# A gated cross attention block on one Trainium2 core: the feed forward of the first three batches is worked into the last two attention units

## The reference

```python
def attention(query, kv):                       # per batch
    q = (query @ Wq + bq).reshape(B, L, 8, 4, 128)
    k, v = jnp.split(kv @ Wkv + bkv, 2, axis=-1)    # 8 heads of 128 each
    scores = jnp.einsum('blkgd,bmkd->bkglm', q, k) * scale
    attn = jax.nn.softmax(scores, axis=-1)
    return jnp.einsum('bkglm,bmkd->blkgd', attn, v).reshape(B, L, 4096) @ Wo + bo

def feed_forward(x):
    base = jnp.einsum('bsd,od->bso', x, base_W)
    probs = softmax(jnp.einsum('bsd,ed->bse', x, router_W))
    top_vals, top_idx = jax.lax.top_k(probs, 2)
    rw = top_vals / sum(top_vals)               # spread to w_dense over the 8 experts
    mid = jnp.einsum('bsd,edr->bser', x, lora_A) * w_dense[..., None]
    return base + 2 * jnp.einsum('bser,erd->bsd', mid, lora_B)

x = x + tanh(g_xattn) * attention(layernorm(x), ctx)
x = x + tanh(g_ffn) * feed_forward(layernorm(x))
```

## Time and profile before

| | us |
|---|---|
| median of 3 runs (lowest to highest) | 2341.92 (2341.48 to 2342.7) |
| the profiled execution | 2345.07 |
| its span in the profile | 2342.9 |
| PE busy | 2292.4 (98%) |
| DVE, ACT, POOL busy | 1827.5, 1686.1, 1622.5 |

### The profile page before, as it was taken

How to read it: one execution, slowest core, us unless ns; L and a number is a source line. 1 busy time by engine, 2 the same in 40 slices (tenths; PEclk the granted TensorE clock), 3 DMA queues, 4 the chain that set the end, 5 groups by cost and what they waited for, 6 DMA issues and landing times.

```text
span 2342.9 us, 37753 instructions
## 1 busy us (share of the span) xinstructions
PE 2292.4 (98%) x12568; PEld 1960.6 (84%) x12568; DVE 1827.5 (78%) x3167; ACT 1686.1 (72%) x3208; POOL 1622.5 (69%) x1367
## 2 busy tenths in 40 slices
PE   7999999999999999999999999999999999999988
PEld 6888888888888888888888888888888888888864
DVE  5887888879778787877778778787878778778775
ACT  4776777767777776777767777776777777777663
POOL 5897887967657786866757777774865667675651
PEclk9999999999999999999999999999999999999999
DMA  7444334454133233335123243323423222122211
GB/s 255 138 145 149 114 126 146 139 194 149 59 124 113 93 122 99 99 107 185 66 97 109 73 133 114 104 89 132 142 65 109 73 72 91 51 85 73 82 37 54
DMA packets 122591, 258.11 MB, mean 110 GB/s; under 512 B 13344, under 2 KB 46624, under 8 KB 122144
## 3 DMA queue, kind: packets, MB, share of 16 engines
q1 hardware_dynamic: 122400, 255.71, 32.3%
HBM read 188.81 MB, written 66.86 MB: 109 GB/s over the span
## 4 chain that ended last, share of the span: by engine, by line
PE 87%; DVE 5%; POOL 4%; ACT 2%; issue 2%; DMA 0%; ACTq 0%; SPq 0%; POOLq 0%; DVEq 0%
PE psW L362 13%; PE psW L363 12%; PE psW L364 12%; PE psW L544 7%; PE psS L364 7%; PE psS L362 7%; PE psS L363 7%; PE psW L546 7%; PE psW L545 7%; PE psW L417 2%; PE psW L425 2%; POOL xs L731 2%; POOL pl L735 1%; PE psW L462 1%; DVE mrun L1132 1%
## 5 line engine op out<-in xcount | busy, mean ns | idle before, releaser
L731 POOL TENSOR_TENSOR xs<-xs,mb 128x512 f32<-128x512 f32 (+1 forms) x832 | 1066.2, 1311 | 535.2 <-ACT mb L795 535.2
L1132 DVE TENSOR_TENSOR mrun<-psS,mrun 128x512 f32<-128x512 f32 (+1 forms) x704 | 483.4, 687 | 379.2 <-ACT xs L795 376.3
L795 ACT ACTIVATE xs<-psS 128x512 f32<-128x512 f32 (+1 forms) x832 | 497.5, 598 | 213.9 <-PE psS L364 204.1
L887 ACT ACTIVATE ph<-xs 128x512 fp32r<-128x512 f32 (+1 forms) x832 | 520.5, 626 | 0.0
L947 DVE TENSOR_TENSOR pl<-psP,ph 128x512 fp32r<-128x512 f32 (+1 forms) x674 | 460.0, 682 | 56.3 <-ACT ph L887 50.5
L1156 DVE TENSOR_TENSOR psum_<-psP,psum_ 128x512 f32<-128x512 f32 (+1 forms) x674 | 457.5, 679 | 0.0
L884 ACT ACTIVATE psP<-xs 128x512 f32<-128x512 f32 (+1 forms) x674 | 403.5, 599 | 3.2 <-DVE psum_ L1156 1.7
L362 PE MATMUL psS<-ql,kh 128*128 128x512 f32 (+1 forms) x832 | 344.7, 414 | 4.2 <-DVE mrun L1132 3.2
L544 PE MATMUL psW<-ph,vh 128*128 128x512 f32 (+1 forms) x832 | 336.1, 404 | 4.5 <-POOL pl L735 3.1
L363 PE MATMUL psS<-qh,kh 128*128 128x512 f32 (+1 forms) x832 | 328.1, 394 | 0.0
L545 PE MATMUL psW<-pl,vh 128*128 128x512 f32 (+1 forms) x832 | 328.1, 394 | 0.0
(11 more groups left out here) (155 smaller groups left out, 4564.0 us busy)
## 6 DMA issues: line engine op xcount, KB each, us to landing
wqh<-scr_wq SPq DMA_DIRECT2D x96, 256.0 KB, 2.6
wql<-scr_wq SPq DMA_DIRECT2D x96, 256.0 KB, 3.0
woh<-scr_wo SPq DMA_DIRECT2D x48, 512.0 KB, 3.2
wol<-scr_wo SPq DMA_DIRECT2D x48, 512.0 KB, 4.3
scr_wq<-wqh SPq DMA_DIRECT2D x32, 256.0 KB, 2.0
scr_wq<-wql SPq DMA_DIRECT2D x32, 256.0 KB, 2.5
scr_wo<-woh SPq DMA_DIRECT2D x16, 512.0 KB, 2.6
scr_wo<-wol SPq DMA_DIRECT2D x16, 512.0 KB, 4.0
```

Source lines behind the costliest of these rows:

```text
L731: eng.tensor_tensor(tile, tile, mb[0:rows_of(t), U % 2, :], ALU.subtract).then_inc(s_sub)
L795: return eng.activation(hi, src, ACT.Copy)
L887: eng.activation(ph[0:rows, T % RP, :], xs[0:rows, T % RX, :], ACT.Exp).then_inc(s_h)
L1132: eng.tensor_tensor(run, psS[0:rows, s % 2, :], a, ALU.max).then_inc(s_m)
```

## The change

- Unit 63 gives its first three tiles to GpSimd, as the units before it do. Their pair lies in the staging tensor `stg`. GpSimd merges unit 62's pair after the subtraction S7 of unit 63, no longer after S1, and DVE adds unit 63's own pair after its last tile.
- Tiles 0 to 5 of the feed forward are normalized, turned and multiplied earlier. GpSimd normalizes tiles 2 and 4. The inverse deviations move two slots forward and ACT's root 13.
- `route` is cut into `route_off`, `route_first`, `route_second` and `route_weights`, done in slots -5, -4, -3 and 0. Most of the intermediate tensors of tiles 0 to 5 lie in a PSUM bank that a transpose in slot -7 opens (job rt) and slot 1 gives back.
- The last row maximum (jobs m, b of unit 63) moves from slots 0 and 2 to slot -1. The base products are spread otherwise: ya0 and yb0 at slots -2 and -1, tiles 3 and 4 between the last spread and after the last output projection.

```diff
     def lead(U):
 
-        return 1 if U < NU or U == UN - 1 else 3
+        return 1 if U < NU else 3
...
     for U in range(UN + 2):
-        for t, names in enumerate((AT[U % 4] if U else "k1 - k2 v0 q0 k3 q1 v1 - v2 - v3 -").split()):
+        names_of = {0: "k1 - k2 v0 q0 k3 q1 v1 - v2 - v3 -", UN: "- - - - - s - r - - o0 - o1",
+                    UN + 1: "- - - - - s - r - - o0 o1"}.get(U, AT[U % 4])
+        for t, names in enumerate(names_of.split()):
...
 
-    for s, names in {-12: "ht0", -10: "ht1 mi0", -9: "ht2 mi1", -7: "ht3 mi2", -5: "ht4 mi3", -4: "ht5 mi4", -2: "mi5",
-                     0: "ga0 ya0", 1: "ga1", 2: "yb0 yl0", 3: "ya1 yb1 yl1 ga2", 4: "ya2", 5: "yb2 yl2 ga3", 6: "ya3",
-                     7: "yb3 yl3 ga4", 8: "ya4", 9: "yb4 yl4", 11: "ga5"}.items():
+    for s, names in {-15: "ht0", -13: "ht1 mi0", -12: "ht2 mi1", -11: "ht3 mi2", -10: "ht4 mi3", -9: "ht5",
+                     -8: "mi4", -7: "mi5 rt0", -2: "ya0", -1: "m yb0 b", 1: "ga0 ya1", 2: "yl0", 3: "yb1 ga1",
+                     4: "yl1", 6: "ya2 ga2", 7: "yb2", 8: "yl2", 9: "ga3", 11: "ga4", 13: "ya3",
+                     21: "yb3 yl3 ya4"}.items():
         for name in names.split():
-            jobs[TN + s].append((name[:2], int(name[2:]), 0))
+            jobs[TN + s].append((name[:2], int(name[2:]), 0) if name[1:] else (name, UN - 1, 0))
...
+        def rt_of(n, k):
+
+            if n == 2 or k in (5, 8):
+                return rt[:, k - 1, 6:8, :] if n == 2 else rt[:, k - 1, 0:6, :]
+            return bank_of(("rt", 0, 0))[:, 48 * k - 48:48 * k].rearrange("p (i e) -> p i e", e=E)
...
                 elif kind == "s":
-                    if lead(n) == 1:
+                    if n == UN - 1:
+                        pe.wait_ge(s_a, a_count[NT * n + NT - 1] + 1)
+                    elif lead(n) == 1:
                         pe.wait_ge(s_a, a_count[NT * n + NT - 1])
                     else:
-                        pe.wait_ge(s_ap, 2 * (n - NU + 1))
+
+                        pe.wait_ge(s_ap, 2 * (n - NU + 1) + (n == UN - 2))
                     turn(("s", n, 0), psum_[:, n % 2, :], s_su, s_r, n + 1)
...
+                if s == TN + 1:
+                    emptied(("rt", 0, 0), s_wt, 6)
                 for j in jobs[s]:
                     job(*j)
-            for name in "ya5 yb5 yl5 ht6 ht7 mi6 mi7 ya6 yb6 ya7 yb7 ga6 yl6 ga7 yl7".split():
+            for name in "yb4 yl4 ga5 ya5 yb5 ht6 ht7 yl5 mi6 mi7 ya6 yb6 ya7 ga6 ga7 yb7 yl6 yl7".split():
...
-                if s == TN - 21:
+                if s == TN - 23:
...
-                "S0,S1 M,S2 L0,S3 L1,S4 L2,S5 A2,S6 S7 S8 S9 S10 S11 S12 -")]
+                "S0,S1 M,S2 L0,S3 L1,S4 L2,S5 A2,S6 S7 S8 S9 S10 S11 S12 -",
+                "S0,S1 S2 L0,S3 L1,S4 L2,S5 A2,S6 S7 M,S8 S9 S10 S11 S12 -")]
             for p in first:
                 cut(*p)
             for s in range(SLOTS):
                 U, t = divmod(s - SUB, NT)
                 if 0 <= U < UN:
-                    for step in steps_at[0 if lead(U) == 1 else 1][t]:
+                    for step in steps_at[0 if lead(U) == 1 else 2 if U == UN - 1 else 1][t]:
                         if step == "M" and U > 0 and lead(U - 1) == 3:
...
-                if s == TN - 8:
-                    pool.wait_ge(s_k, 4 * NK)
-                    pool.wait_ge(s_v, 52 * B)
+                if s in (TN - 14, TN - 11):
+                    i = 2 if s == TN - 14 else 4
+                    pool.wait_ge(s_inv, 3)
+                    pool.wait_ge(s_x1, 16)
+                    pool.wait_ge(s_ht, i - 1)
+                    eng.tensor_scalar(hns[0][:, :], tile_of(i), mv[:, i, 0:1], rstd[:, i:i + 1],
+                                      ALU.subtract, ALU.mult).then_inc(s_hnp)
+                if s == TN - 12:
...
-                if s == NT * (UN - 3) + 1:
+                if s == NT * (UN - 4) + 1:
                     root(3, 0, NQ - 2)
-                if s == TN - 1:
+                if s == TN - 5:
                     route(1)
             root(4, 6, 8)
+            ffn_gated(5)
...
+            def route_of(n):
+                a, z = ((0, 6), (6, 8))[n - 1]
                 shape = [128, z - a, E]
                 bc = lambda ap: ap.unsqueeze(2).to_broadcast(shape)
                 rv = rev[:, :].unsqueeze(1).to_broadcast(shape)
-                R = lambda k: rt[:, k - 1, a:z, :] if k else mid[:, a:z, 128:136]
-                S_ = lambda k: rs[:, k, a:z]
+                R = lambda k: rt_of(n, k) if k else mid[:, a:z, 128:136]
+                S_ = lambda k: rs[:, k, a:z] if n == 2 or k == 5 else bank_of(("rt", 0, 0))[:, 432 + 6 * k:438 + 6 * k]
+                return a, z, bc, rv, R, S_
+
+            def route_off(n):
+                a, z, bc, rv, R, S_ = route_of(n)
                 dve.wait_ge(s_mc, z)
                 dve.wait_ge(s_rev, E)
                 settle(eng.tensor_reduce(S_(0), R(0), X, ALU.max))
                 eng.tensor_tensor(R(1), R(0), bc(S_(0)), ALU.subtract).then_inc(s_dx)
                 dve.wait_ge(s_dx, n)
+
+            def route_first(n):
+                a, z, bc, rv, R, S_ = route_of(n)
+                if n == 1:
+                    dve.wait_ge(s_ex, n)
                 settle(eng.scalar_tensor_tensor(R(4), R(1), 0.0, rv, ALU.is_equal, ALU.mult))
...
+            def route_second(n):
+                a, z, bc, rv, R, S_ = route_of(n)
                 settle(eng.tensor_tensor(R(7), R(6), bc(S_(5)), ALU.is_equal))
...
+            def route_weights(n):
+                a, z, bc, rv, R, S_ = route_of(n)
                 settle(eng.tensor_tensor(R(5), R(5), bc(S_(7)), ALU.mult))
-                settle(eng.tensor_tensor(R(8), R(8), bc(S_(3)), ALU.mult))
-                settle(eng.tensor_tensor(R(9), R(5), R(8), ALU.add))
+                settle(eng.tensor_tensor(R(3), R(8), bc(S_(3)), ALU.mult))
+                settle(eng.tensor_tensor(R(9), R(5), R(3), ALU.add))
                 for i in range(a, z):
                     inner = mid[:, i, 0:128].rearrange("p (e r) -> p e r", e=E)
-                    eng.tensor_tensor(inner, inner, rt[:, 8, i, :].unsqueeze(2).to_broadcast([128, E, 16]),
+                    eng.tensor_tensor(inner, inner, R(9)[:, i - a, :].unsqueeze(2).to_broadcast([128, E, 16]),
                                       ALU.mult).then_inc(s_wt)
...
+                    route_weights(1)
...
+                    if T == TN - 1:
+                        total = psum_[:, UT % 2, :]
+                        dve.wait_ge(s_a, a_count[T])
+                        dve.wait_ge(s_ap, 2 * (UT - NU))
+                        eng.tensor_tensor(total, pair_of(UT)[:, 0, :], total, ALU.add).then_inc(s_a)
...
+                if s == NT * (UN - 4):
                     floored_var(0, NQ - 2)
-                if s == NT * (UN - 3) + 3:
+                if s == NT * (UN - 3) + 1:
                     inverse_dev(3, 0, NQ - 2)
-                if s == TN - NT:
-                    dve.wait_ge(s_x1, 16)
-                    ffn_norm(0)
-                    ffn_norm(1)
-                if s == TN - 1:
-                    route(1, 0, 6)
+                for i in {TN - 18: (0,), TN - 17: (1,), TN - 12: (3,), TN - 10: (5,)}.get(s, ()):
+                    ffn_norm(i)
+                if s == TN - 5:
+                    dve.wait_ge(s_rtb, 1)
+                    route_off(1)
+                if s == TN - 4:
+                    route_first(1)
+                if s == TN - 3:
+                    route_second(1)
...
+            ffn_out(4)
```

More of the change, by code:

```diff
@@ L271, in gated_block @@
         s_hn = sem("s_hn")
+        s_hnp = sem("s_hnp")
+        s_rtb = sem("s_rtb")
+        s_inv = sem("s_inv")
         s_hT = sem("s_hT")
@@ L328, in gated_block, with pair_of @@
                 in_psum.append(T)
+        def pair_of(U):
+            return stg if U == UN - 1 else pp
         def exp_place(T):
@@ L334, in exp_place @@
             if t < lead(U):
[L335 removed]
+                return pair_of(U)[:, t - 1, :]
             return psP[0:rows_of(t), (l_count[T] - 1) % 2, :]
@@ L497, in job @@
                     turn(("x", n, part), src, s_xt, s_xl, i + 1)
+                elif kind == "rt":
+                    eng.transpose(take(("rt", 0, 0))[:, 0:128], ident[:, :], ident[:, :]).then_inc(s_rtb)
                 elif kind == "ht":
-                    pe.wait_ge(s_hn, n + 1)
+                    if n in (2, 4):
+                        pe.wait_ge(s_hnp, n // 2)
+                    else:
+                        pe.wait_ge(s_hn, (0, 1, 3, 5, 6, 7).index(n) + 1)
                     turn(("ht", n, 0), hns[n % 2][:, :], s_ht, s_hT if n < 7 else s_hT7, n + 1 if n < 7 else 1)
@@ L738, in add_p @@
                 pool.wait_ge(s_lp, lp_count[T])
-                eng.tensor_tensor(pp[:, 0, :], pp[:, 0, :], pp[:, 1, :], ALU.add).then_inc(s_ap)
+                pair = pair_of(T // NT)
+                eng.tensor_tensor(pair[:, 0, :], pair[:, 0, :], pair[:, 1, :], ALU.add).then_inc(s_ap)
```

(18 more changed lines are left out.)

18 lines of the change are left out of this document (7 added, 11 removed).

## The result

| kernel | median, us | from, to | runs |
|---|---|---|---|
| before | 2342.68 | 2340.41, 2354.76 | 20 |
| changed | 2346.48 | 2344.44, 2353.68 | 20 |

The ratio is 1.0016, with a 95% interval of 1.0009 to 1.0024: 3.8 us slower. The interval leaves out 1, so the slowing is real, but it lies inside the 0.2% that I had called no change. The profiled executions took 2345.07 us before and 2345.97 us after, with spans of 2342.9 and 2344.1 us. They lie only 0.9 us apart because the one of before was 2.4 us above its own median.

A forecast was written before the change was run, and what follows sets the result against it. PE, busy for 98% of the span, was taken to bound the kernel. Won 21.7 and lost 24.7 us made it 3 us slower: 2348 us profiled, 2344.9 as median; range 2333 to 2351.

The forecast's parts named there:

- inverse deviations: Unit 61: PE's idle time and slow clock go, 5.9 us, less 0.5 for ACT's root in unit 60; won 5.4.
- small waits (d): Small idle times of PE between 2220 and 2260 us go; won 2.1 us.
- waits for banks: Slots -13, -12 and -7, and tiles 3 and 5: earlier normalizing and turning makes PE wait; lost 4.4 us.
- choice in parts: Slots -6 to -1: the experts' choice moves where DVE is full, 19.3 us against PE's 13.3; lost 5.9 us.
- slot 0: After the last maximum is turned, PE no longer waits for the experts' weights; won 8.2 us.
- merge, with clock: Near slot 5 PE idles 11.8 us for GpSimd's late merge, then 2.5 us of low clock; lost 14.3 us.
- end waits: Four waits of PE for `pl` at the very end go; won 1.4 us.
- (c): Before the last output projection PE idles 3.04 us and starts at half pace; 4.6 us with the refill, all won.
- The merge on time: Rival: PE does not wait for GpSimd's merge near slot 5, so 14.3 us stay won: 2330.6 us; chance 0.12.
- The low clock: Rival: after the 11.8 us of idleness PE stays at half clock for longer, 5 us dearer: 2350 us; chance 0.14.
- The small operations on PSUM: Rival: in slots -6 to -1 they collide with GpSimd's subtractions: 2349 us, at full price 2358; chance 0.06.
- Unit 61 did change: Rival denied here: unit 61 stays as it was because the inverse operations still meet GpSimd: 2351 us; chance 0.04.

The follow-up runs named there:

- alone: The kernel before with only the root in unit 60 and the five inverse operations two slots earlier in unit 61: 2338.94 us against 2342.79 before.
- the early merge: The changed kernel with GpSimd's merge of unit 62's pair behind S1 of unit 63 again: 2333.24 us.

## Why the prediction held, step by step

The forecast was +3 us; it was +3.8. The parts, each in PE time:

| step of the prediction | forecast | measured |
|---|---|---|
| inverse deviations | won 5.4 | 4.0 (5.9 less 1.85 in unit 60); alone 3.9 in medians |
| small waits (d) | won 2.1 | gone, 2.1 |
| waits for banks | lost 4.4 | 0.85 + 1.40 + 1.51 = 3.8 |
| choice in parts | lost 5.9 | 5.2 (with the early merge) |
| slot 0 | won 8.2 | no wait there: 8.2 |
| merge, with clock | lost 14.3 | 11.5 + some 1.3 = 12.8 |
| before the last projection | won 4.6 | 4.6 less 1.6 = 3.0 |
| end waits | won 1.4 | 1.4 less 0.8 = 0.6 |

Measured, 17.9 won against 21.9 lost with the 0.1 of the transpose: 4.0, where the profiles from tile 780 on have 3.5. I had 21.7 and 24.7. Both sides were too large, by 3.8 and 2.8 us, and these errors nearly cancel; that the total came within 1 us is in part luck.

**The merge** was the term that decided, and its wait was right in every part: 1.7 us from ga1, ten operations, an idle time of 11.8 forecast and 11.50 found. Only the clock behind it was mis-sized, 1.3 us instead of 2.5. The 1.3 come from the next stretch: from the turn of unit 62's total to that of unit 63's PE takes 22.49 us in the changed kernel and 22.56 with the early merge, and in the latter 1.33 us are a wait. I had carried over 2.5 from unit 61.

**Banks.** The waits on `acc` (slot -13), `nm` (-12) and `rinv` (-7) stand in the trace at 2225.00, 2228.97 and 2244.27, where the order put them:

```profile
2225.00 1.17 PE L463 MATMUL psW<-la_sb,hT 128*128 128x136 f32 x8 [0.85 <-DVE acc L1021]
...
2228.97 0.63 PE L433 MATMUL psW<-ident,hn 128*128 128x128 f32 x4 [1.40 <-DVE nm L1121]
...
2244.27 1.19 PE L463 MATMUL psW<-la_sb,hT 128*128 128x136 f32 x8 [1.51 <-DVE rinv L1143]
```

Only the 0.6 us for tiles 3 and 5 did not come.

**The choice.** I had counted DVE's operations against PE's work, and that count was right. At the price of 0.235 us an operation it was right too. The 1.3 us for hand-overs to ACT was 0.82. In the changed kernel itself PE idles only 2.20 + 1.74 us there. The clock was low in between, and slow matmuls took up 1.3 us that would have been waiting. From the projection o0 to the turn of the maximum PE takes 10.80 us with the low clock, and 10.79 without it in the early merge.

**The root.** "I take 0.5 us" was too low; unit 60 became 1.85 us longer, 1.22 of them a wait. The step that failed is that I asked how busy ACT is, and not who waits for its weights.

**The end.** "The 4.6 us of (c) go": they did, and 1.6 came back. The early merge has the same two short waits there and a full clock, and takes 31.15 us from that turn to the end of the span where the changed kernel takes 32.72.

**The rivals.** The merge on time (2330.6) is the early merge: 2333.2. It lies 2.6 above, of which 1.33 is the wait for `pl` that an early merge causes. The low clock did not last. The small operations on PSUM did not meet GpSimd. In the changed kernel five of them stand in the midst of seven subtractions (2248.99 to 2257.7) and start 0.24 us apart:

```profile
2255.29 0.20 DVE L1090 SCALAR_TENSOR_TENSOR psW<-psW,rev 128x48 f32<-128x48 f32 x1
2255.53 0.22 DVE L1091 TENSOR_REDUCE psW<-psW 128x6 f32<-128x48 f32 x1
```

Unit 61 did change, so that rival is out too. The Trainium skill (Perfetto Trace Analysis, section Optimizing Scalar/DVE Operations) would have them dearer on PSUM than on SBUF; here both start 0.24 us apart, so no run here shows that difference.

## What to carry to other kernels

When an engine's list is rewritten for one purpose, look for every other consumer of a step that it moves: the merge cost PE 1.22 us for each operation put ahead of it, and the three tiles that it made room for saved nothing that the runs could tell. Count a stage by the work of its fullest engine plus the time in which that engine waits for others in its own order. Spreading the work over slots does not lower the first, and moving one hand-over by a slot lowered the second (2.0 us in the profile; the medians do not tell). Ask of a step that stalls an engine (here two table loads) who waits for what that engine makes, not how busy it is.
